# The front of an attention kernel: two buffer sets for the high and low parts, x loaded from ACT's queue, maxima in blocks 5 to 7, V of block 0 ahead of the filter's fold

## What is computed

```
xn  = layernorm(x)
q, k, v = xn @ w_qkv, split in 16 heads of 16
q, k = irfft(rfft(.) * sigmoid(mask_logits))        per head, over its 16 features
attn = softmax(q @ k.T / 4) @ v                      per batch and head, 2048 x 2048
h    = relu(xn @ W_fc.T) ** 2 ;  y = h @ W_proj.T
out  = x + attn @ w_out + b_out + (spikes of 5 steps of a leaky integrator on y) / 5
```

## Time and profile before

| | us |
|---|---|
| median of 3 runs | 1849.54 |
| lowest, highest | 1845.75, 1850.59 |
| the profiled execution | 1849.1 |
| its span in the trace | 1847.3 |
| PE busy | 1816.0 (98% of the span) |
| DVE busy | 1423.0 (77%) |
| ACT busy | 1074.7 (58%) |
| POOL busy | 711.7 (39%) |

### The profile page before, as it was taken

The page is one execution under the profiler, slowest core; times in us unless marked ns, Lnnn a source line. Parts: engine busy times, 40 slices in busy tenths (PEclk is TensorE's granted clock), DMA queues, the critical chain, the costliest instruction groups (busy, mean ns, idle before and its releaser), DMA issues.

```text
span 1847.3 us, 35475 instructions
## 1 busy us (share of the span) xinstructions
PE 1816.0 (98%) x14288; PEld 1091.7 (59%) x14288; DVE 1423.0 (77%) x1781; ACT 1074.7 (58%) x1181; POOL 711.7 (39%) x948
## 2 busy tenths in 40 slices
PE   6889999999999999999999999999999999999998
PEld 4555666555555656555566665555566565555666
DVE  5576778777877788778877787778777877788765
ACT  3325666666666666666666666666666666666662
POOL 1000444433334444433344444333344443333445
PEclk9998999999999999999999999999999999999999
DMA  4752222211222222201222222112222222112223
GB/s 155 221 201 42 44 44 40 42 32 23 42 44 43 44 44 38 43 20 34 44 43 44 44 39 43 30 23 44 44 43 44 44 39 42 20 36 44 43 84 106
DMA packets 85950, 98.81 MB, mean 53 GB/s; under 512 B 50774, under 2 KB 64854, under 8 KB 81690
## 3 DMA queue, kind: packets, MB, share of 16 engines
q1 hardware_dynamic: 85788, 96.56, 23.9%
HBM read 70.80 MB, written 20.99 MB: 50 GB/s over the span
## 4 chain that ended last, share of the span: by engine, by line
PE 94%; DMA 2%; SPq 2%; DVE 1%; issue 0%; ACT 0%; ACTq 0%; DVEq 0%
PE ring L632 31%; PE banks L642 28%; PE ring L622 18%; PE banks L699 6%; PE banks L704 6%; PE ring L783 2%; PE banks L571 1%; SPq L247 1%; PE ring L624 1%; DMA qk_scratch<-hid_sb 1%; DMA attnT<-x 1%; DVE pmax L844 1%; PE ring L562 0%; DMA counts<-wv 0%; PE ring L583 0%
## 5 line engine op out<-in xcount | busy, mean ns | idle before, releaser
L850 DVE TENSOR_REDUCE pmax<-ring 128x2 f32<-128x1024 f32 x1000 | 1176.8, 1218 | 329.0 <-PE ring L624 326.3
L501 ACT ACTIVATE probs<-ring 128x1024 f32<-128x1024 f32 x1024 | 993.4, 1022 | 635.9 <-PE ring L632 635.9
L632 PE MATMUL ring<-qst,kst 66*128 66x512 f32 x2048 | 615.0, 422 | 0.0
L642 PE MATMUL banks<-probs,vst 128*32 128x256 f32 x8192 | 548.7, 385 | 0.1
L632 PEld LDWEIGHTS ring<-qst,kst 66*128 66x128 f32 x2048 | 345.3, 188 | 257.7 <-issue 209.2
L622 PE MATMUL ring<-kst,qst 64*128 64x512 f32 x1000 | 387.8, 467 | 0.0
L624 PE MATMUL ring<-kup,qup 64*128 64x512 f32 x1000 | 387.3, 467 | 0.0
L642 PEld LDWEIGHTS banks<-probs,vst 128*32 128x32 f32 x8192 | 213.8, 109 | 213.7 <-issue 125.1
L421 POOL TENSOR_TENSOR lif<-lif 128x256 f32<-128x256 f32 x32 | 21.7, 677 | 793.3 <-ACT y_sb L517 793.3
L622 PEld LDWEIGHTS ring<-kst,qst 64*128 64x128 f32 x1000 | 183.2, 184 | 159.1 <-DVE pmax L850 82.2
L624 PEld LDWEIGHTS ring<-kup,qup 64*128 64x128 f32 x1000 | 183.1, 183 | 0.0
(11 more groups left out here) (71 smaller groups left out, 681.9 us busy)
## 6 DMA issues: line engine op xcount, KB each, us to landing
qst<-qk_scratch SPq DMA_DIRECT2D x128, 128.0 KB, 4.1
kst<-qk_scratch SPq DMA_DIRECT2D x64, 256.0 KB, 5.9
qup<-qk_scratch SPq DMA_DIRECT2D x252, 64.0 KB, 4.5
qk_scratch<-probs SPq DMA_DIRECT2D x32, 256.0 KB
kup<-qk_scratch SPq DMA_DIRECT2D x64, 128.0 KB, 6.4
attnT<-x SPq DMA_DIRECT2D x8, 512.0 KB, 7.6
qk_scratch<-relu_sb SPq DMA_DIRECT2D x16, 256.0 KB
qk_scratch<-hid_sb SPq DMA_DIRECT2D x16, 256.0 KB
```

The source lines that it names most:

```text
L501: act.activation(probs[:, s % PS, :], score_slot(g), ACT.Exp, scale=SCALE).then_inc(exp_done, 1)
L632: mm = pe.matmul(score_slot(g)[:, c * BLK:(c + 1) * BLK], kst[b][:, kt * P:(kt + 1) * P], qst[b][:, q:q + BLK], start=True, stop=True)
L642: mm = pe.matmul(po[32 * j:32 * (j + 1), half * D:(half + 1) * D], vst[b][:, kt, :], quarters[:, j], start=(kt == 0), stop=(kt == TB - 1))
L850: dve.tensor_reduce(pmax[:, tile, first:first + 2], unit_slot(g).rearrange("p (c e) -> p c e", c=2), AX, ALU.max).then_inc(mx_taken, 1)
```

## The change

- **V of block 0** is projected ahead of the filter's fold; the fold goes to another PSUM slot. Ahead of the first transposes PE does ten matmuls on a tile of zeros.
- **`hilo` has two sets** of four tiles, for even and odd blocks, the second in the unused half of `attnT`. ACT waits for the stores of block t - 2 instead of t - 1. `stored` is a semaphore for each w and set.
- **x of blocks 2 to 7** is loaded from ACT's queue; for block t + 3 behind the copy of the transposes of block t + 1.
- **The first stack** is loaded in two pieces of 1024 tokens (`load_first`), behind the stores of blocks 2 and 4; wfc and the upper keys and queries behind those of block 5.
- **The 48 first maxima** are all in blocks 5 to 7, 16 in each, two in each group of q and k and two in each quarter of v, in an order by pieces (`first_part`).
- **DVE and ACT in block 4** carry the normalisations of blocks 6 (between the low parts) and 7. ACT then does one Exp of one column.
- **SP stores the first shift ahead of block 7's stores**, and behind these come wproj, wout and bout, ahead of the loads for batch 1. PE waits for wfc, wproj and (wout, bout) apart, where they are first used.
- The hardware loops of the front are written out, except POOL's.

Cut to its core:

```diff
+WARM = 10
-AHEAD = [0, 4, 8, 8]
+PIECE = 6 * 16
...
-        hilo = [t.rearrange("p (c t) -> p c t", c=2) for t in
-                (probs[:, 2, :], probs[:, 3, :], relu_sb[:, :, :].rearrange("p f t -> p (f t)"),
-                 hid_sb[:, :, :].rearrange("p f t -> p (f t)"))]
+        hilo = [[t.rearrange("p (c t) -> p c t", c=2) for t in
+                 (probs[:, 2, :], probs[:, 3, :], relu_sb[:, :, :].rearrange("p f t -> p (f t)"),
+                  hid_sb[:, :, :].rearrange("p f t -> p (f t)"))],
+                [attnT[:, 1, w * HALF:(w + 1) * HALF].rearrange("p (c t) -> p c t", c=2) for w in range(QB)]]
...
+        def first_part(n):
+
+            if n < 2 * TB:
+                return n % TB // 2, n // TB * 2 + n % 2
+            return n // 4, n % 4
...
-        stored = [sem(f"stored{i}") for i in range(QB)]
+        stored = [[sem(f"stored{i}_{k}") for k in range(2)] for i in range(QB)]
+        first_in = [sem(f"first_in{i}") for i in range(2)]
...
-            with sp.Fori(0, NB // 4) as n:
-                for p in range(2):
-                    next_x(2 * n + p, p)
-                    store_block(2 * n + p)
-            for t in range(NB // 2, NB):
-                if t < NB - 2:
-                    next_x(t, t % 2)
-                if t == NB // 2:
...
+            def load_first(piece):
+
+                for w in range(QB):
+                    for k in range(2):
+                        sp.wait_ge(stored[w][k], 32 * (piece + 1))
+                cols = slice(piece * HALF, (piece + 1) * HALF)
+                for part in range(2):
+                    for dup in range(2):
+                        r = (2 * part + dup) * DH
+                        sp.dma_start(qst[0][r:r + DH, cols].bitcast(F32), qk_dram[0, 0, part, :, cols]).then_inc(first_in[piece], 16)
+                for dup in range(2):
+                    r = dup * 2 * DH
+                    sp.dma_start(kst[0][r:r + 2 * DH, cols].bitcast(F32),
+                                 qk_dram[1, 0, :, :, cols].rearrange("r d t -> (r d) t")).then_inc(first_in[piece], 16)
+
+            for t in range(NB):
+                store_block(t)
+                if t == 2:
+                    sp.wait_ge(zero_out, 64)
+                    sp.dma_start(qst[0][4 * DH:ROWS, :].bitcast(F32), zero_dram).then_inc(blank_in, 16)
+                    load_first(0)
+                if t == 4:
+                    load_first(1)
+                if t == 5:
+                    sp.dma_start(wfc_sb[:], wfc.rearrange("(c p) e -> p c e", p=P)).then_inc(wfc_in, 16)
+                    load_upper_keys(0, 0)
+                    load_upper_queries(0, 0, 1)
+                if t == NB - 2:
+                    store_shift(0, 0, 0)
+            sp.dma_start(wproj_sb[:], wproj.rearrange("(c p) e -> p c e", p=P)).then_inc(wproj_in, 16)
+            sp.dma_start(wout_sb[:], wout.rearrange("(c p) e -> p c e", p=P)).then_inc(late_in, 16)
+            sp.dma_start(bout_sb[:], bout.partition_broadcast(P)).then_inc(late_in, 16)
             for w in range(QB):
-                sp.wait_ge(stored[w], 32 * (NB + 1))
+                for k in range(2):
+                    sp.wait_ge(stored[w][k], 32 * (NB // 2))
...
+            def load_x(t):
+
+                act.wait_ge(ln_done, t - 1)
+                act.dma_start(x_in[:, t % 2], x_blocks[t]).then_inc(x_landed[t % 2], 16)
+
+            def take_high(t, w):
+                act.wait_ge(qk_ready, QB * t + w + 1)
+                if t > 1:
+                    act.wait_ge(stored[w][t % 2], 32 * (t // 2))
+                act.activation(hilo[t % 2][w][:, 0, :].bitcast(F32R), qk_psum(w), ACT.Copy).then_inc(hi_ready, 1)
...
             take_transposed(0, 0)
+            take_v(0)
 
             act.wait_ge(fold_done, 1)
-            act.activation(wqk_sb, odd_slot.rearrange("p (c e) -> p c e", c=KC), ACT.Copy).then_inc(fold_taken, 1)
+            act.activation(wqk_sb, max_slot.rearrange("p (c e) -> p c e", c=KC), ACT.Copy).then_inc(fold_taken, 1)
             deviation(1)
             act.wait_ge(zero_out, 64)
...
+            load_x(2)
+            for t in range(NB):
+                for w in range(QB):
+                    take_high(t, w)
+                    if t == 4 and w == 1:
+                        deviation(6)
                 if t < NB - 1:
                     take_transposed(t + 1, (t + 1) % 2)
-                if t < NB - 2:
+                if t < NB - 3:
+                    load_x(t + 3)
+                if t < 4:
                     deviation(t + 2)
-                take_v(t)
+                if t == 4:
+                    deviation(7)
+                    act.activation(filt[:, 1, 0:1], filt[:, 0, 0:1], ACT.Exp)
+                if t:
+                    take_v(t)
...
+            pe.wait_ge(preset, 2)
+            for n in range(WARM):
+                pe.matmul(max_slot[:, 0:D], lif[:, 4, 0:P], lif[:, 4, :], start=True, stop=True)
             pe.wait_ge(ident_in, 16)
             transpose_block(0, 0)
+            pe.wait_ge(const_in, 48)
+            pe.wait_ge(xb_ready, 1)
+            project_v(0, 0)
             fold_filter()
             pe.wait_ge(fold_taken, 1)
...
+            for t in range(NB):
+                project_qk(t, t % 2, TB * (t - 5) if t > 4 else None)
                 if t < NB - 1:
                     next_transpose(t + 1, (t + 1) % 2)
-                project_v(t, t % 2, chunk + 2 * QB if units > QB else None)
-                chunk += 2 * units
+                if t:
+                    project_v(t, t % 2, TB * (t - 5) + 8 if t > 4 else None)
...
-            for n in range(chunk, 2 * (UNITS - LEAD)):
-                first_max(n)
-            pe.wait_ge(v_taken, NB + 1)
-            pe.wait_ge(late_in, 64)
+            pe.wait_ge(wfc_in, 16)
...
+            normalise(0)
             build_filter()
-            normalise(1, 0, 1)
...
+            normalise(1)
+            for t in range(NB):
+                for w in range(QB):
+                    if t > 4:
+                        for n in range(2):
+                            first_max(TB * (t - 5) + 2 * w + n)
+                    low_part(t, w)
+                    if t == 4 and w < 3:
+                        (block_stats, block_rstd, block_scale)[w](6)
+                if t < 4:
+                    normalise(t + 2)
+                if t == 4:
+                    normalise(7)
                 if t == NB - 1:
                     for link in range(4):
                         split_shift(link, 0, 0, 2 * TB)
...
+                if t > 4:
+                    for n in range(8):
+                        first_max(TB * (t - 5) + 8 + n)
```

More of the change, by code:

```diff
@@ L245, in store_block @@
                     for part in range(2):
[L246 to L247 removed]
+                        dst = qk_dram[w // 2, g * 8:(g + 1) * 8, part, :, t * BLK:(t + 1) * BLK]
+                        sp.dma_start(dst, hilo[t % 2][w][:, part, :]).then_inc(stored[w][t % 2], 16)
             def load_stack(h, b):
@@ L310, in _ @@
                     load_upper_keys(0, 0)
                     load_upper_queries(0, 0, 1)
[L312 to L320, removed]
@@ L523, in _ @@
             act.wait_ge(xnt_copied, NB + 2)
-            for w in range(QB):
-                act.wait_ge(stored[w], 32 * (NB + 1))
             for s in range(FIRST):
+                if s in (2, 3):
+                    act.wait_ge(stored[s - 2][0], 32 * (NB // 2))
                 if s == 4:
+                    for w in (2, 3):
+                        act.wait_ge(stored[w][0], 32 * (NB // 2))
                     take_up(0, 0, UP_A)
@@ L822, in normalise @@
                 last.then_inc(ln_done, 1)
+            def normalise(t):
+                block_stats(t)
+                block_rstd(t)
+                block_scale(t)
             def build_filter():
@@ L851, in unit_max, with low_part @@
                                   unit_slot(g).rearrange("p (c e) -> p c e", c=2), AX, ALU.max).then_inc(mx_taken, 1)
-            def low_parts(t, n=None):
-                for w in range(QB):
-                    if n is not None:
-                        for c in range(2):
-                            first_max(n + 2 * w + c)
-                    dve.wait_ge(hi_ready, QB * t + w + 1)
-                    dve.tensor_tensor(hilo[w][:, 1, :].bitcast(F32R), qk_psum(w), hilo[w][:, 0, :],
-                                      ALU.subtract).then_inc(lo_done, 1)
+            def low_part(t, w):
+                dve.wait_ge(hi_ready, QB * t + w + 1)
+                dve.tensor_tensor(hilo[t % 2][w][:, 1, :].bitcast(F32R), qk_psum(w), hilo[t % 2][w][:, 0, :],
+                                  ALU.subtract).then_inc(lo_done, 1)
             def split_shift(link, n, half, chunks=None):
@@ L885, in _ @@
             dve.memset(shift[:, 16:32], 0.0).then_inc(shift_blank, 1)
-            normalise(0, 0, 0)
+            normalise(0)
             build_filter()
-            normalise(1, 0, 1)
```

(22 more changed lines are left out.)

77 lines of the change are left out of this document (26 added, 51 removed).

## The result

The changed kernel took 1854.75 us (median of 7 runs) against 1848.76 us of the kernel before beside it: ratio 1.0036, 95% interval 1.0026 to 1.0045. It is **slower**, by some 6 us, 0.36%. The profiled execution has a span of 1854.3 us against 1847.3.

A forecast was written before the change was run, and what follows sets the result against it. PE bounds the kernel (94% of the span), so only the front can give time: s = 8, bound by batch 1's loads, comes at 155.8 against 159.98 (-4.2), plus 2.2 of clock, sum -2.0 us, median 1847.5; range 1839 to 1856.

The forecast's parts named there:

- the wait for DVE's maxima in block 5: Block 5: PE waits 5.6 us for DVE, in place of the 5.9 at 83.45; falling clock costs 2.2 more.
- I take 5.5: Blocks 6 and 7: x from ACT's queue lands in 5.5 us beside stores, with 3.8 and 9.6 as ends.
- the clock behind s = 8: After PE's idle time at s = 8 the clock is low once more: +2.2 us.
- sum of this part: 0: Opening, V ahead of the fold and ten matmuls on zeros: no net change, -2.1 to +3.2 us.
- the ten matmuls of 256 columns take 4.3 us at half speed: Opening: matmuls on zeros run from about 2 us, hidden ahead of the transposes at 10.29; PE then idles 4 us.
- Price and gain nothing: Opening: the matmuls on zeros cost nothing and win nothing, as 4 us of PE idling is expected to undo them.
- V of block 0 at about twice its usual time: Opening, a sign the forecast is right: V at half speed, 6.9 us if throughout, the clock rising after 4.3.
- With 2 us to the first bytes 12.2: Behind block 7: its eight stores, 2.1 MB from 129.8, take 12.2 us (10.2 to 13.6), landing at 142.0.
- I take 2.5: Behind block 7: wproj, wout and bout ahead of batch 1's loads add 2.5 us (0 to 3.7), giving 155.8.
- The slower rival: Blocks 6 and 7: x lands no sooner on ACT's queue than on SP's; +6.2 us, 1855.7; chance 0.12.
- the faster rival: Opening and x: zeros carry the clock, x lands in 3.8 (-1.7), clock stays up; -8.0 us, 1841.5; chance 0.22.
- The Exp table load: Under block 4's wait it frees 1.3 us on ACT before the first scores, which are not the bound.

## Why the prediction was wrong

It forecast 1847.5, 2 us under the kernel before, and the kernel got 6 us slower. Two mechanisms were right: the wait for DVE's maxima in block 5 and the loads of batch 1 as the new bound at s = 8. Terms of the sum were mis-sized: how long x takes to land beside the stores ("I take 5.5", measured 8.3 and 8.4), and how long the stores and weights ahead of batch 1's loads take (12.2 and 2.5, measured 15.6 and 4). Added to the forecast's -2.0, either one alone turns the sign. The result lies inside the range, near its upper end, by the opening's unforeseen gain of 2.1 us: without it the time would be past 1856.

The profiled executions lie +7.0 us apart where the sum had -2.0. The 9 us between, step by step: opening -2.1, x and the clock in blocks 4 and 5 +6.1, from block 7's projection to the first store -0.7, the stores +3.4, loads and weights +1.5, the clock behind s = 8 +0.8.

- **The opening, "sum of this part: 0"**: it gained 2.1 us. The failed step is "the ten matmuls of 256 columns take 4.3 us at half speed", with PE idle for 4 us behind them. I took the duration of one of two instructions for a whole float32 matmul; they took 7.01, PE idled 1.4, and the clock held. "Price and gain nothing" was wrong: without them the projection of block 0 starts 2.9 us later and the median is 4.4 us higher. The sign "V of block 0 at about twice its usual time" did not come (3.69). That block 0 loses its cover was right, and cost 2.0 us in two waits.
- **"I take 5.5"** for x to land from ACT's queue: 8.3 and 8.4, nearer the end of 9.6 that the rival used. This is the first failed step that turns the sign. Each x was issued 3.25 us ahead of its block's projection, not the 2.1 of the forecast, which took back 1.1 of the 2.8 us. PE's waits were 2.4 and 7.3 us where I had 1.0 and 5.6, and the clock fell twice, not once: in block 4 too. Block 5 took 25.63 us (78.87 to 104.50), that is 14.96 and 7.26 and 3.4 of low clock, where I had 2.2. Block 7's projection starts 4.1 us after the 115.4 forecast, 6.1 if the opening's gain is set apart.
- **"With 2 us to the first bytes 12.2"** for block 7's stores: from 133.18 to 148.78 they took 15.6. Issued back to back, eight took SP 8.93 us, 1.1 each, and 15.2 to land with the weights out of the way (133.02 to 148.26), so it is nearly all the stores' own. **"I take 2.5"** for the weights: 4. Together with the late front, 164.07 instead of 155.8. This is the second failed step, 4.9 us. What the order itself costs, the run with the stores first shows: 13.8 us of median.
- **The clock behind s = 8**, 2.2 us: 3.0 (s = 8 to s = 12, against 6.55 us in the kernel before). In six other profiled executions that waited there it was 2.0 to 4.9, so this term alone moves a run by some us.
- **The slower rival** had the right mechanism (x lands hardly sooner on ACT's queue) and nearly the right result, 1855.7, but I gave it 0.12. The nearness is partly luck: it has 8.2 us from x, where 6.1 came, and nothing of the 4.9 behind block 7 or of the 2.1 won in the opening. It also counts the landing twice, for both loads, where the faster rival counts its 1.7 us once. The row against it, that x no longer stands behind eight stores, did not bear what I put on it.
- **"The Exp table load"** and **"SP waits for all of block 7's stores before any such load"** held as written.

Between x on SP's and on ACT's queue the larger part came from issue, 4.4 and 1.6 us against the block's start for the last two loads, against 2.3 and 1.1 of landing. So the rule of the Trainium skill ("Trainium Kernel Development and Optimization", Key Constraints), that a second issuing engine saves only issue time, was nearer than my reading of the idle row; by it alone both would have landed alike.

## What to carry to other kernels

When a front gets shorter, look at what its tail was hiding: here the loads of the next stack had 11 us to spare, and moving one small urgent DMA ahead of 2 MB of stores spent them all. A DMA on a second queue is not past the traffic of the first: look at all that is in flight when it is issued. Put a wait on a DMA queue behind everything that is already ready to go, and issue a load when its buffer falls free, not where the code happens to need the next one. A landing time beside other traffic is not read from a row on idle DMA.

## What the runs showed of the hardware

- 512 KB of x on ACT's queue took 4.1 us on idle DMA (block 2) and 7.9 to 8.5 beside stores that used half of the DMA engines' time (blocks 3 to 7 of the changed kernel).
- 8 KB in four DMAs on ACT's queue took 6.6 us from the last issue (120.6 to 127.16), with stores until 123.04, 1 MB of weights and then 1.57 MB of loads in flight on SP's; on SP's queue, right behind the stores and ahead of the weights, it took 2.2 (121.16 to 123.36). By the Trainium skill ("DMA: Bandwidth & Descriptors", Queues, rings and completion order) the write that raises a DMA's semaphore lands only after every earlier write of the same DMA engine, across its queues. The trace agrees with that, but no run here separates it from the engines' plain sharing.
- A DMA that stands behind an activation in ACT's program was issued when that started, not when it ended: x of block 6 at 60.08, the copy ahead of it from 60.07 to 61.09.
- The clock fell behind a PE wait of 2.4 us in block 4 (0.67 in 74 to 76) as well as behind 7.3 us, and in the run with one set of buffers behind 1.69 us (0.55 in 84 to 86). In the first pairs of the changed kernel, with gaps of 0.3 and 0.4 us, it held at 1.00.
- Eight stores of 256 KB that were all ready took 8.93 us to issue from SP, against 5.99 at 80.38 in the kernel before. No run here tells why.
